# A two-expert-of-eight kernel on one core: the second layer's first block list after two routed steps instead of three

## What is computed

```python
x = L0_attn_x
x = x + 0.5 * ffn(layernorm(x), ...)
x = x + attn(layernorm(x), ...)
x = x + 0.5 * ffn(layernorm(x), ...)      # the same weights

def ffn(x):                                # 4096 tokens, 8 experts, top 2
    normed = layernorm(x) * ln_gamma + ln_beta
    probs = softmax(normed @ router_w.T);  top_v, top_i = top_k(probs, 2)
    gates = softmax(top_v)
    out = sum over e of comb[:, e] * swiglu(normed, gate_up_w[e], down_w[e])   # 384 hidden
    return out + swiglu(normed, shared_gate_up_w, shared_down_w)               # 128 hidden

def attn(x):                               # 32 windows of 128 tokens
    q, k, v = x @ Wq.T + bq, x @ Wk.T + bk, x @ Wv.T + bv
    keep the 32 largest of each row of q k.T / sqrt(128); softmax over them; times v
    leaky relu, + x, layernorm * gamma + beta
```

## Time and profile before

| | us |
|---|---|
| median of three runs (658.46 to 661.5) | 658.55 |
| span of the profiled execution, first to last instruction | 581.5 |
| the median less this span | 77.05 |
| TensorE busy in the span | 500.6 |
| VectorE busy in the span | 388.7 |

### The profile page before, as it was taken

One profiled execution on the slowest core, in us unless ns is written; L12 is line 12 of the kernel. 1 busy time (PEld: TensorE's weight loads), 2 busy tenths in 40 slices (PEclk: granted clock), 3 DMA queues, 4 the chain that ended last, 5 costly groups with the idle time before them and its releaser, 6 DMA issues.

```text
span 581.5 us, 14497 instructions
## 1 busy us (share of the span) xinstructions
PE 500.6 (86%) x3928; PEld 458.6 (79%) x3928; DVE 388.7 (67%) x1688; ACT 330.0 (57%) x792; POOL 332.0 (57%) x491
## 2 busy tenths in 40 slices
PE   2588999989999989999977499996899999799781
PEld 1466999979899989998974369794889989799780
DVE  5558864732558989879887958999785624222574
ACT  3367556565467777667753357673655546555430
POOL 2273766875565675356674405664566765565542
PEclk9989999999999999999977569997999999999996
DMA  6944858766886554766412254431668767676993
GB/s 184 316 112 167 261 188 237 243 233 239 284 260 218 190 187 173 258 226 205 155 47 59 69 195 176 160 112 54 209 224 257 248 221 246 228 262 237 322 320 124
DMA packets 88012, 117.82 MB, mean 203 GB/s; under 512 B 11848, under 2 KB 60880, under 8 KB 87936
## 3 DMA queue, kind: packets, MB, share of 16 engines
q1 hardware_dynamic: 76208, 96.75, 49.8%
q0 software_dynamic: 9312, 19.16, 9.5%
q10 hardware_dynamic: 2416, 0.99, 0.7%
HBM read 26.57 MB, written 26.19 MB: 91 GB/s over the span
## 4 chain that ended last, share of the span: by engine, by line
PE 52%; SPq 15%; ACT 9%; DMA 7%; issue 7%; DVE 5%; POOL 3%; ACTq 1%; POOLq 0%; DVEq 0%
PE ps_y L730 12%; PE ps_g L716 11%; PE ps_u L721 6%; SPq L441 6%; PE ps_h L721 5%; DMA xin<-rows 5%; SPq L484 4%; SPq L479 3%; PE ps_x L711 2%; PE w L630 2%; SPq L499 2%; POOL rows L1572 2%; ACT zz L849 2%; PE w L660 2%; PE w L616 2%
## 5 line engine op out<-in xcount | busy, mean ns | idle before, releaser
L1589 POOL DMA_INDIRECT results<-raw_gu,idx x163 | 164.6, 1010 | 144.8 <-ACT raw_gu L929 103.1
L1572 POOL DMA_INDIRECT rows<-zz,s_idx x128 | 126.0, 984 | 66.9 <-issue 28.3
L730 PE MATMUL ps_y<-dn_t,raw_gu 128*128 x978 | 139.2, 279 | 5.7 <-ACT raw_gu L929 5.0
L716 PE MATMUL ps_g<-x_t,raw_dn 128*128 128x128 f32 x978 | 137.5, 277 | 0.0
L730 PEld LDWEIGHTS ps_y<-dn_t,raw_gu 128*128 128x128 f32 x978 | 123.4, 193 | 9.3 <-issue 8.5
L716 PEld LDWEIGHTS ps_g<-x_t,raw_dn 128*128 128x128 f32 x978 | 122.8, 192 | 3.6 <-issue 3.5
L929 ACT COPY raw_gu<-ps_y 128x128 f32<-128x128 f32 x163 | 42.9, 263 | 103.5 <-PE ps_y L730 101.8
L923 ACT ACTIVATE sil<-ps_g 128x384 f32<-128x384 f32 x163 | 80.1, 491 | 22.0 <-PE ps_g L716 20.8
L920 ACT ACTIVATE x_t<-ps_x,bf_c,gf_c 128x128 f32<-128x128 f32 x163 | 75.3, 462 | 19.6 <-PE ps_x L711 19.4
L1397 DVE TENSOR_TENSOR raw_gu<-sil,ps_u 128x384 f32<-128x384 f32 x82 | 44.9, 548 | 54.2 <-PE ps_u L721 47.2
L1397 DVE TENSOR_TENSOR raw_gu<-sil,ps_h 128x384 f32<-128x384 f32 x81 | 44.5, 550 | 50.8 <-PE ps_h L721 35.9
(11 more groups left out here) (172 smaller groups left out, 729.0 us busy)
## 6 DMA issues: line engine op xcount, KB each, us to landing
raw_dn<-gu_t SPq DMA_DIRECT2D x163, 384.0 KB
xin<-rows SPq DMA_DIRECT2D x163, 64.5 KB
yg<-results SPq DMA_DIRECT2D x15, 512.0 KB, 5.1
results<-raw_gu,idx POOLq DMA_INDIRECT x163
rows<-pads SPq DMA_DIRECT2D x40, 64.5 KB
rows<-pads SPq DMA_DIRECT2D x5, 451.5 KB
rows<-zz,s_idx POOLq DMA_INDIRECT x128, 2.4
out<-xres SPq DMA_DIRECT2D x7, 256.0 KB, 3.3
```

Source lines behind the costliest of these rows:

```text
L716: t = pe.matmul(ps_g[k][:, c, :], ws[:, k4, c * P:(c + 1) * P], x_t[:, k, :], start=True, stop=True)
L730: t = pe.matmul(ps_y[:, 0, :], h_t[:, k4, c * P:(c + 1) * P], dn[:, bass.ds(off + c * D, D)], start=(c == 0), stop=(c == FC - 1))
L1572: pool.indirect_dma_start(xs, bass.IndirectOffsetOnAxis(s_idx[n][:, c, k:k + 1], 0), zz[n][:, k, c, :], None).then_inc(scat[n], 16)
L1589: pool.indirect_dma_start(yt, bass.IndirectOffsetOnAxis(idx[:, ky:ky + 1], 0), yb[:, ky, :], None).then_inc(yst[ky], 16)
```

## The change

`LISTS` decides after which routed steps lists are made. The second layer's first list comes after two steps (9 blocks, 85 to 93), a further one after the third (8 blocks, 94 to 101); the others are as before. There are ten lists in place of nine, the blocks, their number and their rows' layout are the same. The new first list is made as the old first one was, by 15 operations; the list after the third step is now a further one, of 17. Besides, all five `WEAVE` strings are new.

```diff
-LISTS = ((2, 3, 6, 8), (3, 5, 6, 7, 8))
+LISTS = ((2, 3, 6, 8), (2, 3, 5, 6, 7, 8))
...
 WEAVE = {
     "sp": """
-        8 7 3 8 2 2 13 8 24 12 4 45 9 13 12 1 48 9 7 z1 14 22 38 4 4 z1 1 z1 5 z1 3 z6""",
+        8 z1 5 13 1 2 14 3 31 6 4 51 2 7 33 z2 51 3 6 5 2 63 2 7 z2 2 4 z1 1 z6""",
     "pe": """
-        z5 2 2 z1 1 z1 3 z2 1 z1 2 4 2 z2 8 4 3 z2 2 5 4 z1 1 5 2 6 4 z1 6 5 4 z2 98 3 z1 3 6 8 3 z1 5 3 2 3 12 5 z1 5 5 2 5 7 4 4 12 1 22 3 z1 3 z1
+        z4 1 1 4 z2 1 1 z3 1 2 4 4 z2 5 4 6 1 z1 3 3 2 z2 7 2 6 5 1 4 5 2 6 2 91 3 z1 2 1 15 2 z1 4 4 6 3 9 4 2 3 6 3 3 7 4 1 14 3 23 2 z1 3 z1
...
```

More of the change, by code:

```diff
@@ L114 @@
     "sp": """
-        8 7 3 8 2 2 13 8 24 12 4 45 9 13 12 1 48 9 7 z1 14 22 38 4 4 z1 1 z1 5 z1 3 z6""",
+        8 z1 5 13 1 2 14 3 31 6 4 51 2 7 33 z2 51 3 6 5 2 63 2 7 z2 2 4 z1 1 z6""",
     "pe": """
-        z5 2 2 z1 1 z1 3 z2 1 z1 2 4 2 z2 8 4 3 z2 2 5 4 z1 1 5 2 6 4 z1 6 5 4 z2 98 3 z1 3 6 8 3 z1 5 3 2 3 12 5 z1 5 5 2 5 7 4 4 12 1 22 3 z1 3 z1
-        3 3 8 z1 3 z2 6 7 z1 3 2 5 4 2 z1 1 z2 1 z7 1 2 1 z1 3 7 z1 6 1 2 10 5 1 z3 4 9 z1 5 z1 1 5 z3 7 z1 2 3 11 3 3 6 z1 21 5 3 4 z1 22""",
+        z4 1 1 4 z2 1 1 z3 1 2 4 4 z2 5 4 6 1 z1 3 3 2 z2 7 2 6 5 1 4 5 2 6 2 91 3 z1 2 1 15 2 z1 4 4 6 3 9 4 2 3 6 3 3 7 4 1 14 3 23 2 z1 3 z1
@@ L119 @@
+        3 2 8 z1 3 z1 1 4 5 3 4 z1 6 6 1 z4 2 3 z1 3 4 3 2 1 z5 4 z1 2 3 3 4 5 2 4 z2 2 3 3 4 z1 3 2 2 z2 7 z1 4 2 18 3 1 4 z1 20 4 1 4 z1 1""",
     "act": """
-        z12 1 1 z2 1 z1 2 3 z5 1 1 z4 1 6 3 1 z3 1 4 2 2 z4 5 2 z1 3 z3 9 4 2 11 5 56 2 z2 2 3 z1 3 7 z3 3 3 z4 1 4 2 z1 8 z2 1 2 3 1 z4 6 z1 4 4 z1
-        2 z1 2 4 3 z1 1 z2 21 z3 3 2 z1 2 2 z1 5 1 z6 2 z1 2 1 1 4 2 z3 5 2 3 3 z4 1 z2 1 z3 1 1 z15 1 z1 1 1 z1 2 z1 1 z2 8 z1 4 8 z8 1 2 z2 3 2 1
-        z2 4 z1 5 3 z6 3 z3 3 8 z4 2 3 3 15 1 z1 1 4 z1 3 40 15 1""",
+        z13 4 z3 1 3 z6 1 2 z4 2 3 4 3 z4 5 2 z2 1 2 z1 1 6 z5 10 2 5 9 6 56 z2 1 3 3 z1 1 7 z2 2 3 2 z4 1 4 1 4 5 z1 2 1 1 3 2 z4 3 3 3 3 z1 1
@@ L123 @@
+        1 2 3 z1 3 2 z2 21 z1 2 z1 3 1 z1 3 z1 2 3 z7 3 1 2 1 z1 3 3 z3 6 z1 5 5 z15 2 z1 4 3 2 3 z17 4 2 3 4 z3 1 z3 4 z1 1 1 z2 1 2 z2 6 z1 3
+        2 z9 1 8 1 10 z3 3 3 z1 15 z3 3 3 1 9 8 4""",
     "dve": """
-        z153 1 z1 1 z4 1 z20 1 z11 1 z4 1 z5 1 z2 1 z9 1 z16 2 z7 2 z2 1 z9 2 z2 1 z13 1 z3 1 1 z1 1 z2 8 1 3 3 1 z2 1 z5 1 z4 1 z1 1 1 z3 1 z6 1 z5
-        2 z13 1 z9 1 z2 1 z2 1 z7 1 z5 1 1 z10 2 z25 1 z1 1 z2 1 z10 2 z4 1 z7 1 z15 1 z10 1 z6 2 z9 1 1 z4 1 z9 2 z1 1 z13 2 z5 1 z12 1 z10 1 z2 2
@@ L126 @@
-        z20 1 z10 1 z7 2 z4 1 z29 1 z101 1 z3 1 z17 1 z1 1 z3 1 z6 1 z2 1 z10 1 z3 1 z14 1 z17 1 z13 1 z7 1 z15 1 z10 1 z2 1 z46 1 z24 2 z15 1 z5 1
-        z8 1 z24 1 z4 2 z19 1 z1 1 z9 2 z1 2 z30 1 2 z10 9 z5 5 z2 2 z2 9 4 1 3 1 1 z1 1 z3 3 z2 1 1 z2 3 z6""",
+        z141 1 z2 1 z8 1 z16 1 z2 1 z19 2 z4 1 z12 1 z15 1 z1 1 z10 2 z3 1 1 z4 1 z7 1 z6 1 z8 1 z1 1 z5 2 z2 15 z1 1 z4 1 z3 1 z6 1 z1 1 z3 1
+        z7 1 z3 1 z2 1 z13 1 z2 1 z5 1 1 z6 1 z5 1 z3 1 z2 1 z17 1 z14 1 1 z6 1 z8 1 1 z9 1 z2 1 z25 1 z7 1 z2 1 1 z3 1 1 z1 1 z4 1 z9 1 z1 1
@@ L128 @@
+        z7 1 z7 1 z3 1 z13 1 z5 1 z7 1 z5 1 z11 1 z10 1 z4 1 z9 1 z13 1 z23 1 z37 1 z4 1 z70 1 z16 1 1 z3 1 z1 1 z18 1 z1 1 z17 1 z13 1 z11 1
+        z5 1 z7 1 z12 1 z29 1 z33 1 z6 1 z3 1 z11 1 z7 1 z1 1 z8 1 z8 1 z34 1 1 z11 1 z7 1 z1 1 z16 3 z25 1 z14 1 z1 1 z5 3 z2 31 1 z4 2 1 1 z1
+        1 z1 2 z2 1 z6""",
     "pool": """
-        z21 2 1 z1 1 z3 4 z2 3 z1 1 2 z1 5 1 2 2 1 1 3 1 2 z2 1 1 3 3 2 5 16 4 13 4 5 5 z1 5 1 1 2 2 z1 3 z2 2 5 31 z2 3 z1 5 4 z1 2 1 z1 5 1 z3 3
-        z10 8 1 7 z1 2 1 1 1 2 2 z3 6 z4 3 z2 1 3 z1 5 5 1 4 2 2 2 z2 3 7 z3 10 7 1 10 3 3 10 40""",
+        z20 2 z3 1 z1 1 z3 2 3 2 2 z3 3 z1 5 1 z1 2 1 z1 1 4 z1 3 3 1 z1 2 4 1 1 7 3 1 9 1 z1 3 5 2 4 1 z1 3 2 2 4 40 1 3 2 2 z1 2 2 z1 15 z2 1
@@ L131 @@
+        z1 3 z1 3 z1 7 z1 1 z1 1 z2 2 1 2 1 z1 2 3 z2 4 1 4 z1 2 z1 2 z1 1 z1 1 6 z5 4 2 3 4 z1 4 4 z2 2 z1 4 4 2 z2 3 7 6 3 1""",
 }
```

## The result

| | before | after |
|---|---|---|
| median, timed side by side | 659.51 us (658.46 to 661.5, 4 runs) | 686.08 us (680.78 to 690.9, 4 runs) |
| ratio | | 1.0438, interval 1.0352 to 1.0525 |
| profiled execution: device time, span | not given, 581.5 | 690.9, 688.9 |

A forecast was written before the change was run, and what follows sets the result against it. PE was taken as busy after x102, so x102's time moves the end, with DVE the longest part of turns 4 and 5. Terms summed to -0.9 at x102, -1.0 in the tail: 656.6 us, range 650 to 663.5.

The forecast's parts named there:

- to x102: Between routed step 4 and x102: two result scatters between step 4's scatters instead of three, -0.3 us.
- With the 77.05 around it.: Whole kernel: 77.05 us outside the 581.5 us span, added to get the forecast median of 656.6 us.
- All else of the plan ... 0, ±3: First layer, fillings, POOL: parts move by a block or two where PE is busy anyway; 0, +-3 us.
- The further list: End of turn 3: new 9-block list with nothing beside it to fill DVE; +3.9 us, less 0.27, bounds 3.0 to 4.1.
- Before the logits: Turn 4: product d83 moves before step 2's transposes, so DVE's 2.25 us stall shrinks; -1.3 us (0 to -2.25).
- After the shared gate: Turn 4: x86, g85, u85 precede the prefixes and x86 waits for ACT's row copy; +2.0 us (+1.2 to +2.6).
- Turn 5, -3.2: Blocks 86 to 89 at PE's beginning: DVE idle time -4.7 us, values behind three blocks +1.5; sum -3.2.
- the rival: Turns 4 and 5: PE stays fed, clock stays at 2.4 GHz; 649 us, in part 650 to 655; chance 0.35.
- Turn 6, -2.0: Turn 6: two blocks less on PE, two products less on DVE, DVE's busy time holds; -2.0 us (0 to -3.5).
- The tail, -1.0: Last stretch: x159 is issued before the outputs, putting a block in hand; -1.0 us (0 to -3).
- None of the three: Rivals: clock stays up (649 us), block 85's rows late (665), nothing reaches the end (658.5 to 661).
- The one on the far side: Turn 4: PE waits for block 85's late rows, x85 8.0 us late; 665 us; chance of above 661.8, all causes, 0.18.

The follow-up runs named there:

- the control: The kernel before, run again unchanged to get a trace that fits its timed runs: ratio 1.002, median 651.92 us.
- new from turn 4 on: New lists and new plan from attention turn 4 on, old plan before; with 0.36 us POOL filling behind every indirect DMA: 0.9561 of kernel before, 631.84 us.

## Why the prediction was wrong, step by step

From the row numbers of steps 1, 2, 3 and 4 (start of the operation that writes `s_idx`), x102 on PE and the end of the span: the changed kernel less the control (351.2, 391.9, 427.0, 464.9, 490.1, 688.9 less 326.5, 358.2, 395.0, 431.7, 456.0, 653.2), and the same for new from turn 4 on less before, both with 0.36 us behind every indirect DMA (315.7, 350.5, 385.3, 421.2, 443.0, 633.9 less 308.0, 339.6, 377.4, 409.9, 434.7, 618.2).

| stretch | predicted | after less control | from turn 4 on, spaced |
|---|---|---|---|
| up to turn 4 | 0 | +24.7 | +7.7 |
| turn 4 | +4.6 | +9.0 | +3.2 |
| turn 5 | -3.2 | -1.7 | -3.0 |
| turn 6 | -2.0 | +1.2 | +3.4 |
| to x102 | -0.3 | +0.9 | -3.0 |
| behind x102 | -1.0 | +1.6 | +7.4 |

These are single executions; of the last pair the one was the fastest and the other the slowest of its runs, so that their 15.7 us stand for 2.5 by the ratios (0.4 points of 660). Differences of 3 us in one stretch aren't to be leaned on.

**"With the 77.05 around it."** This step failed first. A span 77 us under the median was a sign that the profiled execution wasn't one of those timed, and I took it for a constant outside the span. It is 1.75 us. What was missing in the trace was 89 us of unexplained waits (of the control's chain they are 11.1%, 73 us), and with them most of what makes the changed kernel lose.

**"All else of the plan ... 0, ±3".** This failed most: 24.7 of the 35.7 us in the table are lost before turn 4. The first layer's new plan alone costs 1.8% and that of turns 0 to 3 alone 2.5%. "Moves parts by a block or two in stretches in which PE is busy anyway" leaves out that they also move POOL's scatters. With 0.36 us behind every indirect DMA 2 to 2.3 points still stay with this part. By the chains above much of that may be late hand-overs again, but not in turn 3. With 0.36 us behind every indirect DMA it takes 51.3 us in the changed kernel (269.7 to 321.0, PE busy 45.86) and 43.1 in the kernel before (PE busy 42.52), with 0.4 us of unexplained waits on the chain; with 0.61 us behind the scatters it takes 50.5 us against 43.2, with none in either. So the new order by itself makes this turn 7 to 8 us longer, against a term of 0 for all of it. Which of its orders does that is open; a hint is that the turn takes 49.0 us also in the spaced kernel that is new only from turn 4 on, whose splice changed POOL's order in turn 3.

**"The further list", +3.9.** Right as the length of a step: 3.6 us between the row numbers of steps 1 and 2, and the four wide operations of the list took 0.23 us each in place of 0.30, as estimated. As a price at x102 it was too high, since 2.2 of it are left there and 0.7 at the end.

**Turn 4.** "Before the logits", -1.3: the wait went from 2.25 to 0.85. "After the shared gate", +2.0: from the shared product to the use of the prefixes it is 4.60 us, 4.21 in the spaced kernel, against 3.67; so 0.5 to 0.9, and the term was too high. x86 did wait for ACT, 2.34 us. Together with the list's 3.6 that gives 3.1, and 3.2 was measured with the spacing, though in the spaced pair the parts differ somewhat. Without it the turn lost 9.0; the chain there has 9.5 us of unexplained waits in the changed kernel and none in the control.

**Turn 5, -3.2.** -3.0 with the spacing, by the named mechanism, though in part traded: 3.8 us less for the logits, 3.1 more for the shared gate. The clock went from 0.64 to 0.80, not to 1.00 as the rival had it.

**Turn 6, -2.0.** The sign was wrong: +3.4 and +1.2. I reckoned with PE's and DVE's busy time, which did fall (30.16 to 29.74, 28.18 to 27.61), but the turn isn't set by either. PE is idle 6.2 us of it where it was idle 2.3. The spaced trace shows late hand-overs in this turn too:

```profile
398.07 0.27 ACT L936 COPY raw_gu<-ps_y 128x128 f32<-128x128 f32 x1 [2.72 <-remote]
...
409.34 0.19 DVE L1152 TENSOR_REDUCE m_all<-lg_all 128x4 f32<-128x32 f32 x1 [4.92 <-ACT lg_all L894]
```

Unexplained waits are 6.0 us of the turn's chain, and DVE waits 4.92 us for the logits; the same turn of the kernel before so spaced has neither. Less those 6.0 us the turn would be 2.6 us shorter than before, near the forecast. That is an estimate from the chain: in every trace of the new plan this turn has at least 6 us of such waits on it.

**The tail, -1.0.** Not resolved: +1.6 and +7.4, in single executions, while the runs of one kernel spread over up to 10 us.

**Rivals.** None of the three happened. The one on the far side had the right sign by a wrong mechanism.

What is shown: in the executions that are timed, PE's products are late where POOL's indirect DMAs follow each other unbroken (the wait goes with the space and moves with the scatters). How much of this change's loss is that isn't measured to the point: with 0.61 us behind the scatters 4.4 points become 0.3, with 0.36 us behind all indirect DMAs 2.3, and of the 35.7 us between the two unspaced traces 19 are unexplained waits on the chain (92 us against 73). By these numbers it is about half or more. Against them stands turn 3, which the new order makes 7 to 8 us longer without any late hand-over. What stays open: why the first profiled execution had none of it with the same scatters, whether the product or its signal is late, whether it is POOL's issuing or its DMAs' traffic, and why it reaches PE.

## What to carry to other kernels

Compare the span of a profile with the timed runs before anything is read from it: if they differ by more than the 2 us or so outside the span, take another profile, for the one at hand isn't of an execution like those that are timed. When scatters or gathers on POOL run back to back beside matmuls, look for waits marked "remote" on a single core, and try a pause of some 0.4 us behind each (here 0.36 gave 4.8%, and 0.49 no more, since POOL became part of the chain). A plan that moves them can cost several per cent with the same instructions on every engine but for one short list. And cost a new order of work for every engine that it moves, not for the one that seems to be the bound.

## What the runs showed of the hardware

- A product of PE can be handed over up to 11 us after its recorded end while POOL issues indirect DMAs every 1.26 us (0.96 us each), with PE, ACT and DVE idle (control, 35.58 to 46.66). With a pause of 0.61 us between them that wait was gone. One execution of the same kernel, the first that was profiled, had no such wait anywhere.
- The places come back from run to run: in the control and in the kernel with only the new lists, the first late join waits until 46.66 and 46.63, and ACT's copy before it until 38.81 and 38.80.
- PE's own instructions can be held up as well: in the changed kernel three groups of its weight transposes start at 35.97, 40.13 and 44.38, behind gaps of 1.86, 3.34 and 3.35 us that the trace marks "issue", so without a wait that it shows.
- The page "SBUF — State Buffer" of the Trainium skill, on the two sides of SBUF, has PE and ACT never wait on anyone at SBUF's ports. These runs don't look at the ports, so they neither confirm nor refute that; they show that PE's products can still come late, and that with space between POOL's indirect DMAs most of that is gone.
- POOL's own indirect DMAs took 1.35 to 1.82 us in place of 0.96 at some places of such rows (359.96 in the changed kernel: 1.35).
